# Last expert layer: the 48-row products of the down ranks moved to the lower half of the array and beside the fuse-in, four mid banks in turn made three and one

## The reference, cut to what matters

```python
def _fused_linear(x, W, qa, qb, scale, w):
    out = x @ W.T
    a = jnp.einsum('th,krh->tkr', x, qa)
    b = jnp.einsum('tkr,khr->tkh', a, qb)
    mix = jnp.einsum('tkh,tk->th', b, w)
    return out + scale[None, :] * mix

def expert(muW, gW, gqa, gqb, gs, uW, uqa, uqb, us, dW, dqa, dqb, ds, w):
    xe = x + w @ muW.T
    gate = jax.nn.silu(_fused_linear(xe, gW, gqa, gqb, gs, w))
    up = _fused_linear(xe, uW, uqa, uqb, us, w)
    return _fused_linear(gate * up, dW, dqa, dqb, ds, w)
```

## Time and profile before

| | |
|---|---|
| median of 3 runs | 1079.33 us (1076.84 to 1083.56) |
| profiled execution | 1085.57 us, of which 1083.8 us are the span from first to last instruction |
| mean granted TensorE clock | 0.928 |
| busy | PE 965.6 us (89%), DVE 542.2 (50%), ACT 362.7 (33%), POOL 210.1 (19%) |
| expert part | about 826 us to 1073 us of the span |

### The profile page before, as it was taken

One profiled execution on the slowest core, in us unless ns is written; L12 is line 12 of the kernel. 1 busy time (PEld: TensorE's weight loads), 2 busy tenths in 40 slices (PEclk: granted clock), 3 DMA queues, 4 the chain that ended last, 5 costly groups with the idle time before them and its releaser, 6 DMA issues.

```text
span 1083.8 us, 18888 instructions
## 1 busy us (share of the span) xinstructions
PE 965.6 (89%) x7456; PEld 607.6 (56%) x7456; DVE 542.2 (50%) x1091; ACT 362.7 (33%) x724; POOL 210.1 (19%) x258
## 2 busy tenths in 40 slices
PE   7998779999879999997965599879599999999995
PEld 4665523333458899995444267748465444444443
DVE  2599778887431110105468677545854332323324
ACT  3434336666422233223359145124231100000002
POOL 5021100000012222211024843730000111111110
PEclk9999868999889999998988799987779999999998
DMA  4000500000346455535000201220014133322001
GB/s 163 2 2 1 244 1 2 1 2 2 117 145 231 156 190 166 186 101 202 2 1 2 78 2 40 80 115 27 2 48 108 28 89 89 88 83 72 24 1 39
DMA packets 27067, 79.35 MB, mean 73 GB/s; under 512 B 9940, under 2 KB 16348, under 8 KB 20964
## 3 DMA queue, kind: packets, MB, share of 16 engines
q1 hardware_dynamic: 24772, 72.10, 20.0%
q0 software_dynamic: 2208, 6.03, 1.9%
HBM read 69.57 MB, written 8.55 MB: 72 GB/s over the span
## 4 chain that ended last, share of the span: by engine, by line
PE 71%; DVE 18%; issue 3%; ACT 3%; POOL 2%; DMA 2%; SPq 0%; DVEq 0%; ACTq 0%; POOLq 0%
PE psum L1563 8%; PE psum L1143 8%; PE psum L1155 7%; DVE arena L2144 4%; PE psum L866 3%; PE psum L1567 3%; PE psum L1364 3%; PE psum L1593 3%; PE psum L1551 3%; PE psum L1597 2%; PE psum L1047 2%; PE psum L1529 2%; DVE arena L2063 2%; DVE arena L2062 2%; PE psum L1588 2%
## 5 line engine op out<-in xcount | busy, mean ns | idle before, releaser
L1810 ACT ACTIVATE arena<-psum,arena 128x128 f32<-128x128 f32 x184 | 52.6, 369 | 121.0 <-PE psum L1143 92.4
L1999 ACT ACTIVATE arena<-psum 128x512 f32<-128x512 f32 (+1 forms) x32 | 19.0, 593 | 219.5 <-PE psum L1567 219.5
L2144 DVE TENSOR_REDUCE arena<-psum 128x2 f32<-128x512 f32 x128 | 82.6, 688 | 17.4 <-PE psum L993 15.3
L1563 PE MATMUL psum<-arena 128*128 128x512 f32 (+1 forms) x192 | 90.6, 608 | 0.5 <-DVE arena L2603 0.5
L1143 PE MATMUL psum<-arena 128*128 128x128 f32 x736 | 88.8, 280 | 0.0
L1143 PEld LDWEIGHTS psum<-arena 128*128 128x128 f32 x736 | 86.2, 196 | 2.7 <-issue 2.7
L792 POOL TENSOR_TENSOR arena<-arena 128x512 f32<-128x512 f32 (+1 forms) x32 | 40.5, 1265 | 234.8 <-ACT arena L1999 234.8
L1155 PE MATMUL psum<-arena 128*128 x368 | 83.4, 378 | 0.0
L2287 DVE COPY arena<-psum 128x256 f32<-128x256 f32 x23 | 9.8, 425 | 139.9 <-PE psum L1128 89.4
L1786 ACT ACTIVATE arena<-psum 128x1024 f32<-128x1024 f32 x64 | 65.5, 1025 | 37.5 <-PE psum L1015 35.0
L1155 PEld LDWEIGHTS psum<-arena 128*128 128x128 f32 x368 | 67.9, 189 | 9.0
(11 more groups left out here) (354 smaller groups left out, 1796.9 us busy)
## 6 DMA issues: line engine op xcount, KB each, us to landing
arena<-in_w SPq DMA_DIRECT2D x31, 1024.0 KB, 9.0
arena<-in_experts SPq DMA_DIRECT2D x8, 1248.0 KB, 6.3
arena<-mixed SPq DMA_DIRECT2D x16, 256.0 KB
arena<-mixed SPq DMA_DIRECT2D x8, 512.0 KB, 9.4
arena<-returned SPq DMA_DIRECT2D x8, 256.0 KB, 4.9
kept<-arena SPq DMA_DIRECT2D x2, 1024.0 KB, 7.8
arena<-kept SPq DMA_DIRECT2D x2, 1024.0 KB, 6.7
arena<-in_w_ffn SPq DMA_DIRECT2D x1, 1152.0 KB, 5.1
```

The costliest lines, as they stand in the source:

```text
L1563: pe.matmul(out, e[w][:, k, :], xe6[:, half, k, :], start=(k == 0), stop=False)
L1810: last = act.activation(hidt[:, r % 2, ic * P:(ic + 1) * P], bank(n)[:, i * P:(i + 1) * P], ACT.Gelu, bias=b1_tile[:, r % 4, ic:ic + 1])
L2144: ax_max.by(dve.tensor_reduce(nmx[:, b % 2, :, h], bank(u % 2).rearrange("p (t s) -> p t s", t=2), AX.X, ALU.max, negate=True))
```

## The change

The 48 tail rows move from partitions 0 to 47 to 64 to 111 (`dqat`, `dwx`, `ha6`), and the weighted down ranks from partitions 64 to 127 to 0 to 63. The two products over the tail rows become a function of their own, `tail_ranks(n)`, which opens the accumulation and is issued right behind the next step's fuse-in, ahead of the features; `outputs` closes it with the 128-row part. The products with DVE or ACT as readers now take banks 0 to 2 in turn, and the down ranks have bank 3 alone.

```diff
-        order = list(ring)
+        mid_banks = [[key for key in ring if key[0][0] != "d"][i::3] for i in range(3)] + [[key for key in ring if key[0][0] == "d"]]
...
         def bank_free(pe, key):
 
-            if ring[key] >= 4:
-                before = order[ring[key] - 4]
+            users = next(keys for keys in mid_banks if key in keys)
+            if key != users[0]:
+                before = users[users.index(key) - 1]
...
+            def tail_ranks(n):
+                e, half = ex[n // 2 % BUFS], n % 2
+                bank_free(pe, (("d", 0), n))
+                pe.wait_ge(mid_dve.sem, mid_dve.base + by_dve[("t", 0), n] + 1)
+                for u in range(2):
+                    pe.matmul(mid_bank(("d", 0), n)[64 * u:64 * u + 64, 0:D], e["dqat"][64:64 + TAIL, :],
+                              ha6[64:64 + TAIL, half, u * D:(u + 1) * D], start=True, stop=False,
+                              tile_position=(64, 64 * u), skip_group_check=True)
+
             def outputs(n):
                 e, half = ex[n // 2 % BUFS], n % 2
                 key = (("d", 0), n)
-                bank_free(pe, key)
-                pe.wait_ge(mid_dve.sem, mid_dve.base + by_dve[("t", 0), n] + 1)
-                for i in range(2):
-                    for u in range(2):
-                        cols = slice(u * D, (u + 1) * D)
-                        last = pe.matmul(bank(ring[key] % 4)[64 * u:64 * u + 64, 0:D], e[("dqa", "dqat")[i]],
-                                         (h6[:, half, cols], ha6[0:TAIL, half, cols])[i],
-                                         start=(i == 0), stop=(i == 1))
+                for u in range(2):
+                    last = pe.matmul(mid_bank(*key)[64 * u:64 * u + 64, 0:D], e["dqa"], h6[:, half, u * D:(u + 1) * D],
+                                     start=False, stop=True, skip_group_check=True)
                 mid_ps.by(last)
...
             for step in range(STEPS + 1):
                 if step + 1 < STEPS:
                     fuse_in(step + 1)
+                if step >= 1:
+                    tail_ranks(step - 1)
                 if 0 <= step < STEPS:
                     features(step)
...
-                    last = dve.tensor_tensor(out=ha6[64:P, half, cols], in0=bank(ring[("d", 0), n] % 4)[rows, 0:D],
+                    last = dve.tensor_tensor(out=ha6[0:64, half, cols], in0=mid_bank(("d", 0), n)[rows, 0:D],
```

More of the change, by code:

```diff
@@ L68 @@
           ("qb", P, (P + TAILS,)), ("qs", P, (P + TAILS,)), ("dw", P, (D,)), ("dwx", P, (D,)),
-          ("dqa", P, (KX * RX,)), ("dqat", TAIL, (KX * RX,)), ("ds", P, (D,)), ("mu", 32 + KX, (P,))]
+          ("dqa", P, (KX * RX,)), ("dqat", 64 + TAIL, (KX * RX,)), ("ds", P, (D,)), ("mu", 32 + KX, (P,))]
 def columns(parts):
@@ L530, in build, with mid_bank @@
                     by_act[(kind, 0), step] = len(by_act)
-        order = list(ring)
+        mid_banks = [[key for key in ring if key[0][0] != "d"][i::3] for i in range(3)] + [[key for key in ring if key[0][0] == "d"]]
+        def mid_bank(*key):
+            return bank(next(i for i in range(4) if key in mid_banks[i]))
         def bank_free(pe, key):
-            if ring[key] >= 4:
-                before = order[ring[key] - 4]
+            users = next(keys for keys in mid_banks if key in keys)
+            if key != users[0]:
+                before = users[users.index(key) - 1]
                 if before in by_dve:
@@ L1543, in fuse_in @@
                     rows = slice(32 * k, 32 * k + KX)
-                    mid_ps.by(pe.matmul(bank(ring[("x", k), n] % 4), ex[f % BUFS]["mu"][rows, :], wm6[rows, f % BUFS, cols],
+                    mid_ps.by(pe.matmul(mid_bank(("x", k), n), ex[f % BUFS]["mu"][rows, :], wm6[rows, f % BUFS, cols],
                                         start=True, stop=True))
@@ L1550, in ranks @@
                 for k in range(KC):
-                    last = pe.matmul(bank(ring[("a", 0), n] % 4), ex[n // 2 % BUFS]["qa"][:, k, :], xe6[:, n % 2, k, :],
+                    last = pe.matmul(mid_bank(("a", 0), n), ex[n // 2 % BUFS]["qa"][:, k, :], xe6[:, n % 2, k, :],
                                      start=(k == 0), stop=(k == KC - 1))
@@ L1560, in from_x @@
                     bank_free(pe, key)
-                    out = bank(ring[key] % 4)[0:m, :]
+                    out = mid_bank(*key)[0:m, :]
                     for k in range(KC):
@@ L1998, in _ @@
                         act.wait_ge(sh_h.sem, sh_h.base + 2 * len(SHARED))
-                    mid_act.by(act.activation(g6[dst, 2 * (n % 2) + i, :], bank(ring[(kind, 0), n] % 4)[src, :],
+                    mid_act.by(act.activation(g6[dst, 2 * (n % 2) + i, :], mid_bank((kind, 0), n)[src, :],
                                               ACT.Silu))
@@ L2585, in inputs6 @@
                         dve.wait_ge(mid_ps.sem, mid_ps.base + ring[("t", 0), n - 2] + 1)
-                    do(dve.tensor_tensor(out=xe6[:, half, k, :], in0=bank(ring[("x", k), n] % 4),
+                    do(dve.tensor_tensor(out=xe6[:, half, k, :], in0=mid_bank(("x", k), n),
                                          in1=xt[:, k, half * BANK:(half + 1) * BANK], op=ALU.add), mid_dve)
@@ L2593, in inputs6 @@
                     do(dve.tensor_tensor(out=qb6[:, f % 2, :], in0=e["qb"], in1=e["qs"], op=ALU.mult), qb6_ready)
-                    do(dve.tensor_tensor(out=e["dwx"][64:P, :], in0=e["dwx"][64:P, :], in1=e["ds"][64:P, :],
+                    do(dve.tensor_tensor(out=e["dwx"][0:64, :], in0=e["dwx"][0:64, :], in1=e["ds"][0:64, :],
                                          op=ALU.mult), qb6_ready)
             def hidden6(n, i):
-                kind, src, rows = (("u", slice(0, P), P), ("t", slice(64, 64 + TAIL), TAIL))[i]
+                kind, rows = (("u", slice(0, P)), ("t", slice(64, 64 + TAIL)))[i]
                 dve.wait_ge(mid_ps.sem, mid_ps.base + ring[(kind, 0), n] + 1)
@@ L2602, in hidden6 @@
                     dve.wait_ge(out6_ps.sem, out6_ps.base + 4 * (n - 1))
-                do(dve.tensor_tensor(out=(h6, ha6)[i][0:rows, n % 2, :], in0=g6[src, 2 * (n % 2) + i, :],
-                                     in1=bank(ring[(kind, 0), n] % 4)[src, :], op=ALU.mult), mid_dve)
+                do(dve.tensor_tensor(out=(h6, ha6)[i][rows, n % 2, :], in0=g6[rows, 2 * (n % 2) + i, :],
+                                     in1=mid_bank((kind, 0), n)[rows, :], op=ALU.mult), mid_dve)
             def ranks6(n):
@@ L2610, in ranks6 @@
                 dve.wait_ge(mid_ps.sem, mid_ps.base + ring[("a", 0), n] + 1)
-                do(dve.tensor_tensor(out=aw6[:, half, :], in0=bank(ring[("a", 0), n] % 4),
+                do(dve.tensor_tensor(out=aw6[:, half, :], in0=mid_bank(("a", 0), n),
                                      in1=we6[:, f % BUFS, half * BANK:(half + 1) * BANK], op=ALU.mult), mid_dve)
@@ L2790 @@
             "qb": fused(unrank("L1_ffn_gate_qb", f), unrank("L1_ffn_up_qb", f)), "qs": fused(*scales),
-            "dw": dw[:P], "dwx": np.concatenate([dw[P:], np.zeros((64 - TAIL, D), np.float32), unrank("L1_ffn_down_qb", f)]),
-            "dqa": dqa[:P], "dqat": dqa[P:], "ds": every(g["L1_ffn_down_scale"][f]),
+            "dw": dw[:P], "dwx": np.concatenate([unrank("L1_ffn_down_qb", f), dw[P:], np.zeros((64 - TAIL, D), np.float32)]),
+            "dqa": dqa[:P], "dqat": np.concatenate([np.zeros((64, KX * RX), np.float32), dqa[P:]]), "ds": every(g["L1_ffn_down_scale"][f]),
             "mu": np.concatenate([mu[:, :P], np.zeros((32 - KX, P), np.float32), mu[:, P:]])}))
```

## The result

| | before | changed |
|---|---|---|
| median, 20 runs each | 1079.28 us | 1085.81 us |
| ratio of the changed to the kernel before | | 1.0062, 95% interval 1.0042 to 1.0083 |
| profiled span, mean granted clock | 1083.8 us, 0.928 | 1082.9 us, 0.932 |
| expert part: first pass of features(0) to the start of the last matmul | 237.9 us | 244.9 us |
| a half expert, from fuse-in to fuse-in, n = 4 to 15 | 15.04 us | 15.27 and 15.30 in turn |

The change costs 6.5 us (4.5 to 9.0 by the interval). The two spans say the opposite, 1083.8 and 1082.9: the expert part begins at 835.5 in one execution and at 827.5 in the other, in code that the change leaves alone. So the part itself is what two traces can be compared by; it is 7.0 us longer.

The account below looks back on a forecast made before the run. PE was taken to bound the kernel; tails moved cancel (16 x (-0.58 + 0.58) = 0), 3.5 us for the wait before L1597 and 0.8 for step 15 give 4.3 more: 1083.6 us, range 1074.5 to 1088.0.

Parts of the forecast that it names:

- What bounds the kernel: In the stretch of 14 of 16 half experts, PE alone bounds: a microsecond off PE is one off the end.
- The tails behind the fuse-in, 0.58: Tails run 0.58 us behind the fuse-in, cancelling the 0.58 that outputs sheds; bounds 0 to 0.58.
- The wait before L1597, 0.25 x 14 = 3.5: PE waits for DVE's L2619 before L1597, mean 0.25 us in half experts 0 to 13: 3.5 us more.
- Step 15, 0.8: Without a fuse-in, the tails stand between L1597 and L1563 and add 0.8 us.
- Rival (a): Tails run beside the fuse-in in steps 2 to 14: 7.5 us less, 1076.1 us; chance 0.21.
- Steps 1 and 16: First tail's wait existed already and outputs(0) gives back 0.58; in step 16 parts change places: both cost zero.
- The new waits: Waits of tail_ranks on DVE's earlier tail, and of u, t and the next ranks under three banks, cost nothing.
- (d), the clock: PE's new idle time lowers the clock, at 0.88 over 210 us some 25 us; chance 0.04 together with others.
- (b): No wait arises before L1597, only step 15 adds: 1080.1 us; chance 0.09.
- (c): A tail's two token blocks run one after the other in the lower half: 6.9 us, 1090.5 us; chance 0.06.

Follow-up runs that it names:

- 32-row: Changed kernel with the tails' products as 32 rows by 128 columns, 16 of 48 rows left out: half experts 14.70 and 14.73 us, ratio 1.0000.
- upper-half: Changed kernel's order and banks with tails in partitions 0 to 47 as before: half experts 15.27 and 15.30 us, one run of 1087.1 us.

## Why the prediction was right, and where a step of it failed

The time came out at 1085.81 us against 1083.6, inside the range, and the sign and nearly all of the mechanism were right: the 4.3 us forecast were two thirds of the measured 6.5. The terms that were forecast came out one by one; what is missing are two that its sum did not have, the bank and the clock.

- *What bounds the kernel*: PE without a hole in this stretch. Each 0.58, 0.25 or 0.15 us that a run put on PE or took off it was found again in the half expert's length.
- *The tails behind the fuse-in, 0.58*: 0.58, start to start, in every step. The choice between the ends 0 and 0.58 was made by L1069, and the 32-row and upper-half runs bear out the reason: in this place the shape decides and the partitions do not. The rule of the Trainium skill that speaks against the change ("TensorEngine Tiling (Array Packing)", Key Properties: changing the tiling mode, and not just the tile, drains the array) agrees with both runs. The overlap that the Trainium skill's "TensorE: Matmul & The Clock Gate", Part 3, describes for other row groups is there between 8*128 and 32*128, where the features begin 1.07 us after the fuse-in, and is not there between 8*128 and 48*64, which cost their 0.58 us.
- *The wait before L1597, 0.25 x 14 = 3.5*: 0.23 and 0.26 in turn, 3.4 in sum. It was read from the end of L2619, the 0.05 of the signal and the 0.10 of the exposed load, and turning DVE's order takes it away.
- *Step 15, 0.8*: 0.8.
- *Rival (a), 13 x 0.58 = 7.5 less*: its condition did not come, and its price was nearly right. The 32-row run, where it holds, has 236.2 us against the 243.2 of the changed kernel without a fall of the clock, 7.0 less.
- *Steps 1 and 16, "Both are zero"*: this step failed for step 1, by 1.15 us. The prediction saw that `tail_ranks(0)` has to wait for L2603, and held that nothing else changes ahead of it. But in the first round the banks had not yet had a down rank among their users. The old order gave the two products of the third fuse-in the banks of the first gate and the first up; three in turn give them those of the first up and the first tail. So the fuse-in, which had filled the time of that wait, stands behind it. *The new waits, "All free of cost"*, has the same fault: u, t and a were followed in a late step, and the fuse-in, whose banks are the same as before from step 2 on, was not followed in the first.
- *(d), the clock*: given little, and priced for the whole stretch because of the 0.25 us waits. With these waits the clock stayed at 1.00 (855.42 to 1038.79). What happened is smaller and of another place: 1.7 us in step 1, behind a gap that the prediction did not see, in two of seven traces.

With the bank term in it the forecast would have been 4.3 + 1.15, about 5.4 us, or 1084.8; the traces without a fall of the clock show 243.2 - 237.9 = 5.3. If the fall comes in two executions of seven it adds 0.5 to the mean. The sum of 5.8 lies in the measured interval of 4.5 to 9.0. Whether the rest up to 6.5 is anything but the spread of the runs stays open; no trace shows a place for it.

Of the rivals, (a) is out by the timeline, (b) by the half experts of 15.27 and 15.30 us, which go back to 15.04 when DVE's order is turned, and (c) since the two first passes of the tails start together, one row of two records:

```profile
1009.28 0.43 PE L1589 MATMUL psum<-arena 48*64 48x256 f32 x2
```

## What to carry to other kernels

Before work is moved beside other work on PE, compare the shapes and not the partitions. Here 32*128 was hidden beside 8*128, while 48*64 beside the same product cost its full time and a change of shape, on disjoint partitions as on shared ones. Two sizes can count as one shape: 8 and 32 rows ran together, and products of 112 and of 128 columns follow each other without a gap (L1571, two passes in 0.86 us, then L1555). Behind each other a change of the rows alone (128*64 to 48*64) cost 0.15 us, and one of the columns alone (128*128 to 128*64) had the same gap of 0.09 us. Padding the 48 rows with zeros to the neighbour's 128 was worth 0.15 us per change saved, and the added rows cost no time. And when a ring of buffers is cut differently, follow its first round as well as a late one: who is the previous user of each place before all kinds of users have appeared.

## What was not expected of the hardware

A gap of 1.67 us on PE, in a stretch otherwise busy throughout, was followed by a fall of the granted clock from 1.00 to 0.50 in two of seven traces and by none in five; the same kernel showed both. The fall began 2.5 us after the end of the gap (840.9 against 838.43) and doubled the passes for 3.4 us. Gaps of 0.52 and 0.61 us in the same place were followed by none, in the five traces that have them, nor was the gap of 1.36 us in step 15 of five traces, up to the last matmul some 7 us after it. Four passes over 128 rows took no longer than four over 48: the group is 1.01 us long instead of 1.16, shorter by about the gap of 0.09 and the first load of 0.05. And two products of 8 rows and two of 32 on other partitions ran through in the 1.07 us that the two of 8 rows take alone.
